# Window attention on one core: P times V with V stationary in four column groups, P streamed in fp32, and the products in another order

## The chip, the core and the metric

The kernel runs on one core of a Trainium2 chip. The core has a matrix engine (PE, or TensorE, whose weight loads the profile lists apart as PEld), a vector engine (DVE), an activation engine (ACT), a general engine (POOL, or GpSimd) and a queue for transfers (SP). They run independently, each through its own list of instructions in order, and wait for each other on semaphores. The metric is the device time of one execution in microseconds.

## The reference

```python
def _L0_conv_ref(x, qkv_w, qkv_b, proj_w, proj_b):      # WH, WW = 7, 11; 8 heads of 24 channels
...
    xw = xw.reshape(Bnw, N, C)                           # N = 77 tokens in a window
    qkv = xw @ qkv_w + qkv_b
    q, k, v = jnp.split(qkv, 3, axis=-1)
...
    attn = jnp.einsum('bhnd,bhmd->bhnm', q, k) / jnp.sqrt(jnp.float32(hd)).astype(q.dtype)
    attn = jax.nn.softmax(attn, axis=-1)
    out = jnp.einsum('bhnm,bhmd->bhnd', attn, v)
    out = out.transpose(0, 2, 1, 3).reshape(Bnw, N, C)
    out = out @ proj_w + proj_b
...
x = x + _L0_conv_ref(_gn(x), ...)                        # x: (8, 56, 88, 192) fp32; _gn: group norm, 32 groups
```

An image of 56x88 positions with 192 channels is cut into windows of 7x11 positions. There are 8 images and 512 windows. All values are fp32.

## The kernel before

The statistics of the group norm come first: the whole input is read once. Then the main part works on one pair of windows at a time. This is one slot; there are 256. 16 windows (8 pairs, two strips of 8 windows) make a block of 14 image rows, which is loaded and stored as one. A loop of 14 turns holds 16 slots each (two blocks); the first and the last 16 slots, and those that fill and drain the pipeline, are written out around it.

The order of the work is written by hand. Each engine has a function `slot(base, s)` that issues its share of slot s, with `reach(engine, semaphore, count)` ahead of each step; steps of other pairs stand in the same slot, shifted by constants (`AV_LAG` and so on). In slot s PE does, in this order: the scores q k of pair s with q_hi and k_hi alone (`ps_s`, for the row maximum), the k projection of pair s+1 for the first four heads (`qk_projection(ps_k, 1, 0, ...)`), P times V of pair s-2 for its first window (`attention_output`), six transposes of o of pair s-4, k of s+1 for the other four heads, P times V for the second window, four matmuls that add the negated row maxima as one more row to q (`ps_q<-ident_aug,neg_max`), the output projection of a tile or two (`ps_b<-wp`), the transposed scores in three products, q of s+1, V of s+1 (`ps_a<-wv`), and transposes of the normalised input x further ahead (`ps_b<-ident,x_split`).

A matmul in fp16 takes one pass, so fp32 precision is made from two halves: a value is rounded to fp16 (`_hi`) and the remainder kept as a second fp16 (`_lo`), and a product is the sum of three: hi hi, hi lo, lo hi. `products` issues such a group of matmuls, so nearly all matmuls have its line, L676. Making the halves is the work of the other engines: DVE makes q_hi, q_lo, k_lo, v_hi and v_lo, ACT makes k_hi and p_hi (p is the exponential of the scores), POOL makes p_lo, and both halves of o and of x are shared between ACT and POOL.

P times V has P stationary, 77 tokens by 128 columns, and moves the 25 columns of one head of V, the last of them ones, so that the row sum comes out beside the head; three matmuls for each of 16 (window, head), 48 in all. DVE then takes the reciprocal of 16 row sums for each token (L617, 77x16), multiplies (L619), ACT and POOL split o into halves, PE transposes it, ACT copies the transposed halves to `oT`, and the projection takes them as its stationary operand. POOL adds the projection's bias to y beforehand (L370), DVE adds the product to y (L627).

The result of P times V and V itself share the bank `ps_a`; x transposes, o transposes and the projection share `ps_b`.

Of the kernel before, what the change touches and what calls it, by code (L numbers as in the profile page):

```python
# [27 lines left out]
F16 = mybir.dt.float16  # L28
# [34 lines left out]
AV_LAG = 2  # L63
O_LAG = AV_LAG + 1
T_LAG = O_LAG + 1
P_LAG = PAIRS + O_LAG
Y_LAG = PAIRS - 1
V_BUFS = 4
FULL = 128
PAD = FULL - TOK  # L70
AUG_ONE = 32768.0
# [5 lines left out]
def window_attention(nc, x, qkv_w, qkv_b, proj_w, proj_b, out):  # L77
# [4 lines left out]
    with ExitStack() as ctx:  # L82
# [10 lines left out]
        ones = sb("ones", [128, PART])  # L93
        wA, wB = sb("wA", [CA, 3 * CH]), sb("wB", [128, 3 * CH])
        pA, pB = sb("pA", [CA, CH]), sb("pB", [128, CH])
# [3 lines left out]
        wp = {k: sb(f"wp_{k}", [128, CH], F16) for k in PARTS}  # L99
        b_qk, aug, zeros = sb("b_qk", [128, 4]), sb("aug", [128, 4]), sb("zeros", [128, 4])  # L100
        bvA, bvB, b_proj = sb("bvA", [CA, 1]), sb("bvB", [CB, 1]), sb("b_proj", [1, CH])
        bvA_rep, bvB_rep = sb("bvA_rep", [CA, PART]), sb("bvB_rep", [CB, PART])
        bias_out = sb("bias_out", [PART, CH])
# [19 lines left out]
        oT = [sb(f"oT{p}", [128, 3, TILES, PART], F16) for p in range(2)]  # L123
# [8 lines left out]
        v_hi = [sb(f"v_hi{p}", [TOK, 2 * HEADS, HD + 1], F16) for p in range(V_BUFS)]  # L132
        v_lo = [sb(f"v_lo{p}", [TOK, 2 * HEADS, HD + 1], F16) for p in range(V_BUFS)]
        neg_max = sb("neg_max", [TOK, 4, NG, ROW_G], F32R)
        probs = sb("probs", [TOK, NG * 4 * TOK])
        p_hi = [sb(f"p_hi{p}", [TOK, NG * 4 * TOK + PAD], F16) for p in range(2)]
        p_lo = [sb(f"p_lo{p}", [TOK, NG * 4 * TOK + PAD], F16) for p in range(2)]
        recip = sb("recip", [TOK, 2 * HEADS, 1])
        o_sb = [sb(f"o_sb{p}", [TOK, 2, CH]) for p in range(2)]
        o_split = sb("o_split", [TOK, 2, 2 * CH], F16)  # L140
# [6 lines left out]
        ps_b16 = ps_b[:, :].bitcast(F16)  # L147
# [4 lines left out]
        pe_av, pe_oT, pe_proj, pe_xT = sem("pe_av"), sem("pe_oT"), sem("pe_proj"), sem("pe_xT")  # L152
        act_k, act_exp, act_xT = sem("act_k"), sem("act_exp"), sem("act_xT")
        act_p, act_o, act_oT, act_x = sem("act_p"), sem("act_o"), sem("act_oT"), sem("act_x")
        dve_max, dve_q_hi, dve_q = sem("dve_max"), sem("dve_q_hi"), sem("dve_q")
        dve_k, dve_v_hi, dve_v = sem("dve_k"), sem("dve_v_hi"), sem("dve_v")
        dve_norm, dve_recip = sem("dve_norm"), sem("dve_recip")
        dve_out = sem("dve_out")
        pool_p, pool_o, pool_x, pool_y = sem("pool_p"), sem("pool_o"), sem("pool_x"), sem("pool_y")
# [4 lines left out]

        dma_w, dma_bqk, dma_stat = sem("dma_w"), sem("dma_bqk"), [sem("dma_stat0"), sem("dma_stat1")]
# [40 lines left out]
        def xT_psum(c):  # L206
            at = 3 * c * PART
            return ps_b16[:, at:at + 3 * PART].rearrange("p (k v r) -> p k v r", k=3, v=WINS)

        def oT_tokens(buf, chunk, pair):  # L210

            v = oT[buf][:, chunk, :, :].rearrange("p c (v r) -> p v c r", v=WINS)
            return v[:, 2 * pair:2 * pair + 2, :, :]

        def oT_psum(chunk):
            at = 2 * chunk * TOKE
            return ps_b16[:, at:at + 2 * TOKE].rearrange("p (w n) -> p w n", w=2)[:, :, 0:TOK]\
                .rearrange("p w (c r) -> p w c r", c=WIN_W)
# [13 lines left out]
        def _(sp):  # L232
# [3 lines left out]
            sp.dma_start(pA[:, :], proj_w[0:CA, :]).then_inc(dma_w, 16)  # L236
            sp.dma_start(pB[0:CB, :], proj_w[CA:CH, :]).then_inc(dma_w, 16)
            sp.dma_start(pB[CB:128, :], proj_w[CA:CH, :]).then_inc(dma_w, 16)
            v_bias = qkv_b[2 * CH:3 * CH].rearrange("(c a) -> c a", a=1)
            sp.dma_start(bvA[:, :], v_bias[0:CA, :]).then_inc(dma_w, 16)  # L240
            sp.dma_start(bvB[:, :], v_bias[CA:CH, :]).then_inc(dma_w, 16)
            sp.dma_start(b_proj[:, :], proj_b.rearrange("(a c) -> a c", a=1)).then_inc(dma_w, 16)

            sp.wait_ge(pool_const, 6)
            qk_bias = qkv_b[0:2 * CH].rearrange("(sj g d) -> g d sj", g=NG, d=HD)
            for g in range(NG):
                sp.dma_start(b_qk[ROW_G * g:ROW_G * g + HD, :], qk_bias[g, :, :],
                             allow_slow_non_contiguous=True).then_inc(dma_bqk, 16)
                sp.dma_start(aug[ROW_G * g:ROW_G * g + HD, 2:4], zeros[ROW_G * g:ROW_G * g + HD, 0:2])\
                    .then_inc(dma_bqk, 16)  # L250
# [8 lines left out]
            for h in range(2):  # L259
                load_half(0, h, 0)  # L260
            with sp.Fori(1, BATCH) as b:
# [48 lines left out]
        def _(pool):  # L310
# [7 lines left out]
            pool.wait_ge(pool_const, 6)  # L318
# [18 lines left out]
            def slot(base, s, image):  # L337
                i = base + s
                if exists(i - 1):

                    reach(pool, act_p, i)
                    reach(pool, pe_av, i - 2)
                    nc.gpsimd.tensor_tensor(p_lo[(s - 1) % 2][:, 0:16 * TOK], probs[:, :], p_hi[(s - 1) % 2][:, 0:16 * TOK],  # L343
                                            ALU.subtract).then_inc(pool_p, 1)
                if exists(i - O_LAG):

                    reach(pool, act_o, i - O_LAG + 1)
                    nc.gpsimd.tensor_tensor(o_split[:, :, CH:2 * CA], o_sb[(s - O_LAG) % 2][:, :, CA:CH], o_split[:, :, CA:CH],
                                            ALU.subtract)
                    nc.gpsimd.tensor_tensor(o_split[:, :, 2 * CA:3 * CA], o_sb[(s - O_LAG) % 2][:, :, 0:CA], o_split[:, :, 0:CA],  # L350
                                            ALU.subtract).then_inc(pool_o, 1)
# [8 lines left out]
                if exists(i + NORM_LEAD) and (s + NORM_LEAD) % PAIRS == 0:  # L360

                    reach(pool, dma_x[ahead % 2], base + 16 * (ahead // 2) + 16)
                if exists(i - Y_LAG):

                    r = s - Y_LAG
                    if r % PAIRS == 0:
                        reach(pool, dma_y[parity(r)], base + (r // SLOTS) * 16 + 16)
                    y = x_step(y_blk, r)
                    bias = bias_out[:, :].unsqueeze(1).broadcast_to([PART, STEP_TILES[r % PAIRS][1], CH])
                    nc.gpsimd.tensor_tensor(y, y, bias, ALU.add).then_inc(pool_y, 1)  # L370
# [21 lines left out]
        def _(act):  # L392
# [5 lines left out]
            def slot(base, s):  # L398
                i = base + s
                if exists(i - 1):  # L400

                    reach(act, act_exp, i)
                    reach(act, pe_av, i - 2)
                    nc.scalar.activation(p_hi[(s - 1) % 2][:, 0:16 * TOK], probs[:, :], ACT.Copy).then_inc(act_p, 1)  # L404
                if exists(i - T_LAG):

                    o = s - T_LAG
                    reach(act, pe_oT, i - T_LAG + 1)
                    for chunk in range(3):
                        last = nc.scalar.activation(oT_tokens(parity(o), chunk, o % PAIRS), oT_psum(chunk), ACT.Copy)  # L410
                    last.then_inc(act_oT, 1)
                if exists(i - O_LAG):

                    reach(act, dve_norm, i - O_LAG + 1)
                    nc.scalar.activation(o_split[:, :, 0:CH], o_sb[(s - O_LAG) % 2][:, :, :], ACT.Copy)\
# [435 lines left out]
```

## Time and profile before

| | us |
|---|---|
| median of 2 runs | 2115.62 (2107.02 to 2124.22) |
| the profiled execution | 2107.97 |
| its span | 2105.9 |
| mean granted clock of TensorE, 1 is 2.4 GHz | 0.937 |
| first exponential of the scores starts at | 213.0 |
| last one starts at | 2069.7 |

The profile is one execution. Its span is the time from the first to the last instruction; the execution is 2.1 us longer. Up to 160 us DVE reads the input for the statistics and PE has next to nothing to do; from 213 us on all engines repeat the slot.

### The profile page before, as it was taken

The page shows a single profiled execution, that of the slowest core. Times are in us where ns is not written, and L with a number is a line of the kernel's source. Part 1 is how long each engine was busy: PE and PEld are TensorE (multiplying, and loading weights), DVE is VectorE, ACT ScalarE, POOL GpSimd, SP SyncE. Part 2 cuts the span into 40 slices and gives each one's busy share as a digit, 9 for nine tenths or more (in the row PEclk, how much of TensorE's full clock was granted, in tenths as well). Part 3 has the DMA queues.
Part 4 walks back from the last instruction along what each step waited for, and adds up shares of the span by engine and source line. Part 5 has one row for each costly group of instructions (what it writes and reads, how often), then busy time and mean ns, then how long its engine had stood idle before and what let it go on. Part 6 is the DMA issues. An engine that isn't in the chain of part 4 may idle for free.

```text
span 2105.9 us, 97027 instructions
## 1 busy us (share of the span) xinstructions
PE 1691.6 (80%) x41742; PEld 1500.7 (71%) x41742; DVE 1515.2 (72%) x3672; ACT 1299.1 (62%) x2659; POOL 1608.9 (76%) x2060
## 2 busy tenths in 40 slices
PE   0003899988898888988898989988898889988886
PEld 0002788877787778877787878777787778887775
DVE  6772677777677776777777777777777777777783
ACT  0002667767676676766676766766676666767763
POOL 0004689888888898888888998988888888988864
PEclk9999899999999998999999998999999999999996
DMA  6881101111111111111111111111111111111110
GB/s 159 226 232 39 45 20 51 46 57 40 38 57 57 56 57 57 42 54 40 41 54 57 57 57 57 57 39 57 39 50 46 57 57 57 57 48 48 39 39 38
DMA packets 17134, 127.74 MB, mean 61 GB/s; under 512 B 1921, under 2 KB 2178, under 8 KB 2434
## 3 DMA queue, kind: packets, MB, share of 16 engines
q1 hardware_dynamic: 16770, 121.91, 17.1%
q8 instruction: 348, 5.70, 1.1%
q14 instruction: 16, 0.13, 0.0%
HBM read 91.62 MB, written 30.28 MB: 58 GB/s over the span
## 4 chain that ended last, share of the span: by engine, by line
PE 58%; DVE 26%; issue 10%; DMA 3%; ACT 1%; POOL 1%; DVEq 1%; SPq 0%; ACTq 0%; POOLq 0%
PE ps_a L676 25%; PE ps_q L676 8%; PE ps_q L775 6%; PE ps_k L676 6%; PE ps_s L715 6%; DVE v_lo L587 5%; DVE v_hi L641 5%; DVE q_lo L588 5%; DMA x_stat<-in_x 3%; PE ps_b L761 3%; DVE y_blk L627 2%; PE ps_b L676 2%; DVE q_hi L634 2%; DVE k_lo L588 2%; DVE stat L541 2%
## 5 line engine op out<-in xcount | busy, mean ns | idle before, releaser
L343 POOL TENSOR_TENSOR p_lo<-probs,p_hi 77x1232 f16<-77x1232 f32 x256 | 646.8, 2526 | 220.2 <-ACT p_hi L404 217.0
L434 ACT ACTIVATE probs<-ps_s,exp_shift,exp_scale 77x1232 f32<-77x1232 f32 x256 | 351.8, 1374 | 258.1 <-PE ps_s L715 246.1
L676 PE MATMUL ps_a<-v_hi,p_hi 77*128 77x25 f16 x4096 | 362.8, 174 | 84.6 <-DVE v_lo L587 81.9
L676 PEld LDWEIGHTS ps_a<-v_hi,p_hi 77*128 77x128 f16 x4096 | 330.1, 97 | 124.4 <-issue 122.0
L588 DVE SCALAR_TENSOR_TENSOR q_lo<-ps_q,b_qk,q_hi 128x154 f16<-128x154 f32 x512 | 170.4, 376 | 327.9 <-PE ps_q L775 327.9
L596 DVE TENSOR_REDUCE neg_max<-ps_s 77x16 fp32r<-77x1232 f32 x256 | 365.8, 1429 | 34.5 <-PE ps_s L730 34.5
L676 PE MATMUL ps_a<-v_hi,p_lo 77*128 77x25 f16 x4096 | 361.6, 174 | 0.0
L676 PE MATMUL ps_a<-v_lo,p_hi 77*128 77x25 f16 x4096 | 361.2, 174 | 0.0
L676 PEld LDWEIGHTS ps_a<-v_lo,p_hi 77*128 77x128 f16 x4096 | 323.3, 97 | 0.0
L676 PEld LDWEIGHTS ps_a<-v_hi,p_lo 77*128 77x128 f16 x4096 | 321.8, 97 | 0.0
L404 ACT ACTIVATE p_hi<-probs 77x1232 f16<-77x1232 f32 x256 | 310.0, 1211 | 0.3
L376 POOL TENSOR_TENSOR x_norm<-x_norm,mean_all 112x192 f32<-112x192 f32 (+1 forms) x256 | 165.9, 648 | 162.4 <-DVE rstd_all L581 162.4
L442 ACT ACTIVATE xT<-ps_b 128x336 f16<-128x336 f16 x352 | 171.5, 522 | 182.6 <-PE ps_b L829 182.6
L410 ACT ACTIVATE oT<-ps_b 128x154 f16<-128x154 f16 x768 | 181.5, 324 | 146.6 <-PE ps_b L761 144.8
L676 PE MATMUL ps_a<-wv_hiA,xT 128*128 128x192 f16 x1024 | 230.3, 263 | 0.0
L676 PE MATMUL ps_k<-xT,wqk_hiA 128*128 128x154 f16 x1024 | 198.7, 241 | 13.1 <-ACT xT L442 13.1
L378 POOL TENSOR_TENSOR x_norm<-x_norm,rstd_all 112x192 f32<-112x192 f32 (+1 forms) x256 | 166.0, 649 | 48.7 <-POOL x_norm L376 48.7
L634 DVE TENSOR_SCALAR q_hi<-ps_q,b_qk 128x154 f16<-128x154 f32 x512 | 167.8, 369 | 48.6 <-PE ps_q L676 48.4
L676 PE MATMUL ps_q<-xT,wqk_hiA 128*128 128x154 f16 x1024 | 200.5, 248 | 0.0
L715 PE MATMUL ps_s<-q_hi,k_hi 25*128 25x77 f16 x4096 | 145.9, 203 | 59.9 <-DVE q_lo L588 54.5
L370 POOL TENSOR_TENSOR y_blk<-y_blk,bias_out 112x192 f32<-112x192 f32 (+1 forms) x256 | 189.2, 740 | 0.0
L588 DVE SCALAR_TENSOR_TENSOR k_lo<-ps_k,b_qk,k_hi 128x154 f16<-128x154 f32 x512 | 168.0, 371 | 27.6 <-ACT k_hi L421 27.6
(147 smaller groups left out, 5693.5 us busy)
## 6 DMA issues: line engine op xcount, KB each, us to landing
x_stat<-in_x SPq DMA_DIRECT2D x16, 1848.0 KB, 9.9
x_norm<-in_x SPq DMA_DIRECT2D x32, 924.0 KB
y_blk<-in_x SPq DMA_DIRECT2D x32, 924.0 KB
out<-y_blk SPq DMA_DIRECT2D x32, 924.0 KB
wA<-in_qkv_w SPq DMA_DIRECT2D x1, 288.0 KB
wB<-in_qkv_w SPq DMA_DIRECT2D x2, 144.0 KB
pA<-in_proj_w SPq DMA_DIRECT2D x1, 96.0 KB
pB<-in_proj_w SPq DMA_DIRECT2D x2, 48.0 KB
```

What stands on the lines that cost most here:

```text
L343: nc.gpsimd.tensor_tensor(p_lo[(s - 1) % 2][:, 0:16 * TOK], probs[:, :], p_hi[(s - 1) % 2][:, 0:16 * TOK], ALU.subtract).then_inc(pool_p, 1)
L370: nc.gpsimd.tensor_tensor(y, y, bias, ALU.add).then_inc(pool_y, 1)
L378: nc.gpsimd.tensor_tensor(x4, x4, of_group(rstd_all, b, n), ALU.mult).then_inc(pool_norm, 1)
L404: nc.scalar.activation(p_hi[(s - 1) % 2][:, 0:16 * TOK], probs[:, :], ACT.Copy).then_inc(act_p, 1)
L410: last = nc.scalar.activation(oT_tokens(parity(o), chunk, o % PAIRS), oT_psum(chunk), ACT.Copy)
L434: nc.scalar.activation(probs[:, :].rearrange("p (g a n) -> p g a n", g=NG, a=4), scores(), ACT.Exp, bias=exp_shift[0:TOK, :], scale=exp_sc ...
L442: last = nc.scalar.activation(xT_tokens(parity(s + X_LEAD), t0 + c), xT_psum(c), ACT.Copy)
L588: return nc.vector.scalar_tensor_tensor(out=dst, in0=psum, scalar=bias, in1=hi, op0=ALU.add, op1=ALU.subtract)
L596: nc.vector.tensor_reduce(neg_max[:, :, :, HD:HD + 1].rearrange("p a g e -> p g (a e)"), scores(), AXIS.X, ALU.max, negate=True).then_inc( ...
L634: last = ts(by_window(q_hi, j), by_window(ps_q, j), b_qk[:, j:j + 1], None, ALU.add)
L676: last = mm(dst, lhsT, rhs, start=first and n == 0, stop=closes and n == len(pairs) - 1, skip_group_check=True)
L715: last = mm(ps_s[:, g, at:at + TOK], k[rows(g), a:a + FULL], q[rows(g), a:a + TOK], start=n == 0, stop=n == 2)
```

## The change

**P times V.** V is made in fp32 in one copy by ACT (`v_all`, 32 columns for each head: 24 of V, a one, seven zeros). It is now the stationary operand, 77x32, and P moves in fp32, 77 columns. The four heads g = 0 to 3 of a half go to the PSUM partitions 32g to 32g+31, each its own column group of the array. The result is o transposed, with channels on partitions, for both windows 308 columns. Since the row sum is needed on every partition, `denominators` multiplies a block of ones by P as well: eight matmuls that move 154 columns each, into `ps_b`.

**After it.** DVE takes the reciprocal of 128x308 sums and multiplies 128x308; ACT rounds the product into `oT_hi`, POOL makes `oT_lo`. There is no transpose of o any more, and P is no longer split. The projection takes three products for each half of the heads, six matmuls for a tile where there were five. Its bias comes in with the matmul: two spare rows of `wp_hi` hold it, against the ones and their remainder. POOL's addition of the bias is gone.

**The order.** P times V is one slot behind (`AV_LAG` 1, was 2), whole, after q of the next pair. Both halves of k stand behind the scores. V of pair s, not s+1, is made in slot s, ahead of the neg_max matmuls, and the projection stands ahead of V. The transposes of x go to k's bank. On DVE the reciprocal and the product stand first in the slot.

```diff
-AV_LAG = 2
+AV_LAG = 1
...
-                        last = products(ps_a[:, h * (HD + 1):(h + 1) * (HD + 1)], (
-                            (p_hi[p_now][:, at:at + FULL], v_hi[v_now][:, h, :]),
-                            (p_hi[p_now][:, at:at + FULL], v_lo[v_now][:, h, :]),
-                            (p_lo[p_now][:, at:at + FULL], v_hi[v_now][:, h, :])))
+                        at = (2 * w + j) * TOK
+                        o = ps_a[ROW_G * g:ROW_G * (g + 1), 2 * j * TOK:2 * (j + 1) * TOK]\
+                            .rearrange("p (c w r) -> p c w r", c=WIN_W, w=2)[:, :, w, :]
+                        last = mm(o, v_all[s % V_BUFS][:, HEADS * w + NG * j + g, :], probs[s % 2][:, g, at:at + TOK],
+                                  start=True, stop=True, skip_group_check=True)
+                return last
+
+            def denominators(s):
+
+                for w in range(2):
+                    for g in range(NG):
+                        d = ps_b[ROW_G * g:ROW_G * (g + 1), 0:NUM].rearrange("p (a w r) -> p a w r", w=2, r=WIN_H)
+                        last = mm(d[:, :, w, :], ones[0:TOK, 0:ROW_G], probs[s % 2][:, g, 2 * w * TOK:2 * (w + 1) * TOK],
+                                  start=True, stop=True, skip_group_check=True)
                 return last
```

On DVE, at the head of the slot, where the neg_max reduce stood first:

```diff
+                if exists(i - O_LAG):
+
+                    reach(dve, pe_av, i - O_LAG + 1)
+                    reach(dve, act_oT, i - O_LAG - 1)
+                    reach(dve, pool_oT, i - O_LAG - 1)
+                    nc.vector.reciprocal(den_inv[:, :], ps_b[:, 0:NUM]).then_inc(dve_recip, 1)
+                    reach(dve, dve_recip, i - O_LAG + 1)
+                    tt(o32[(s - O_LAG) % 2][:, :], ps_a[:, 0:NUM], den_inv[:, :], ALU.mult).then_inc(dve_norm, 1)
```

On PE, ahead of k, ahead of the projection, and around P times V:

```diff
+                    if exists(i - 1 + X_LEAD):
+
+                        reach(pe, act_xT, i + X_LEAD)
                     reach(pe, dve_k, i + 1)
                     qk_projection(ps_k, 1, 0, s + 1)
...
+                    if exists(i - O_LAG):
+                        reach(pe, dve_recip, i - O_LAG + 1)
...
+                    reach(pe, dve_norm, i - O_LAG + 1)
...
+                if exists(i - AV_LAG):
+
+                    reach(pe, act_exp, i - AV_LAG + 1)
+                    if exists(i):
+                        reach(pe, act_v, i + 1)
...
+                    attention_output(s - AV_LAG, 0)
+                    attention_output(s - AV_LAG, 1)
+                    if exists(i - P_LAG):
+                        reach(pe, dve_out, i - P_LAG + 1)
...
+                    denominators(s - AV_LAG).then_inc(pe_av, 1)
```

PE's list in one slot, from the end of P times V to the transposed scores (`ps_s<-q`; `ps_b<-wp` is the projection), before:

```order
L676 MATMUL ps_a<-v_lo,p_hi 128x25
L676 MATMUL ps_a<-v_hi,p_lo 128x25
L775 MATMUL ps_q<-ident_aug,neg_max 128x78 x4
L676 MATMUL ps_b<-wp_hiA,oT 112x192
...
L676 MATMUL ps_b<-wp_loB,oT 112x192
L715 MATMUL ps_s<-q_hi,k_hi 128x77 x4
```

and the same place after:

```order
L654 MATMUL ps_a<-wv_hiB,xT 128x192
L654 MATMUL ps_a<-wv_loB,xT 128x192
L766 MATMUL ps_q<-ident_aug,neg_max 128x78 x4
L701 MATMUL ps_s<-q_hi,k_hi 128x77 x4
```

Between neg_max and the transposed scores the projection stood, and now nothing does; V stands in front of neg_max. The end of the slot after, from q of the next pair over P times V (`ps_a<-probs`) and the row sums (`ps_b<-probs`) to k:

```order
L654 MATMUL ps_q<-xT,wqk_loB 128x2x77
L678 MATMUL ps_a<-probs,v_all 32x11x7 x16
L174 REGISTER_ALU
L687 MATMUL ps_b<-probs,ones 32x22x7 x8
L174 REGISTER_ALU x2
L808 MATMUL ps_k<-ident,x_split 128x112 x3
L716 MATMUL ps_s<-k_hi,q_hi 128x77 x16
L654 MATMUL ps_k<-xT,wqk_hiA 128x2x77
```

Before, V stood behind q and the two halves of P times V stood around the second half of k; now they are one piece of 24 matmuls in V's old place. DVE's list for one slot, before:

```order
L596 TENSOR_REDUCE neg_max<-ps_s 77x4x4
L588 SCALAR_TENSOR_TENSOR q_lo<-ps_q,b_qk,q_hi 128x2x77 x2
L588 SCALAR_TENSOR_TENSOR k_lo<-ps_k,b_qk,k_hi 128x2x77 x2
L617 RECIPROCAL recip<-ps_a 77x16
L619 TENSOR_TENSOR o_sb<-ps_a,recip 77x384
L627 SCALAR_TENSOR_TENSOR y_blk<-ps_b,out_scale,y_blk 112x384
L634 TENSOR_SCALAR q_hi<-ps_q,b_qk 128x2x77 x2
L641 CAST v_hi<-ps_a 77x16x24
L587 TENSOR_TENSOR v_lo<-ps_a,v_hi 77x16x24
```

and after:

```order
L585 RECIPROCAL den_inv<-ps_b 128x308
L587 TENSOR_TENSOR o_1<-ps_a,den_inv 128x308
L591 TENSOR_REDUCE neg_max<-ps_s 77x4x4
L600 SCALAR_TENSOR_TENSOR y_blk<-ps_b,out_scale,y_blk 112x192
L575 SCALAR_TENSOR_TENSOR q_lo<-ps_q,b_qk,q_hi 128x2x77 x2
L575 SCALAR_TENSOR_TENSOR k_lo<-ps_k,b_qk,k_hi 128x2x77 x2
L621 TENSOR_SCALAR q_hi<-ps_q,b_qk 128x2x77 x2
```

Reciprocal and product moved from behind k_lo to ahead of the neg_max reduce and have 308 columns; the two operations on V are gone.

## Rows read from the trace of the kernel before

**Rows 1.** The page: busy time by engine, and the clock in 40 slices.

```profile
PE 1691.6 (80%) x41742; PEld 1500.7 (71%) x41742; DVE 1515.2 (72%) x3672; ACT 1299.1 (62%) x2659; POOL 1608.9 (76%) x2060
...
PEclk9999899999999998999999998999999999999996
```

**Rows 2.** Chain of waits in order of time, one slot: start, us, what.

```profile
1206.77 0.48 PE ps_q L775 x4
...
1208.01 0.60 PE ps_s L715 x48
1208.61 0.79 PE ps_q L676 x10
1209.40 0.94 PE ps_a L676 x10
...
1210.36 0.57 DVE v_hi L641
...
1210.95 0.57 DVE v_lo L587
...
1211.65 0.76 PE ps_a L676 x24
1212.41 0.22 PE ps_b L761 x6
1212.63 0.34 PE ps_k L676 x5
1212.97 0.60 PE ps_a L676 x24
1213.57 0.48 PE ps_q L775 x4
```

**Rows 3.** The exponential's line: ns min/median/max, first and last start in us.

```profile
L434 ACT ACTIVATE probs<-ps_s,exp_shift,exp_scale x256: 1373/1374/1377, 213.0 to 2069.7; 77x1232 f32<-77x1232 f32 x128
```

**Rows 4.** Timeline of PE at a turn of the loop: start, us, what.

```profile
437.98 0.32 PE L730 MATMUL ps_s<-k_hi,q_hi 25*128 25x77 f16 x16 [3.33 <-issue]
```

**Rows 5.** Busy time by engine in three stretches; PEclk is the granted clock.

```profile
435.00:438.00 3.00, 0.03 (x4) 0.06 (x8) 0.53 (x1) 1.66 (x3) 2.82 (x4) 1.00 0.02 5
441.60:445.00 3.40, 3.40 (x66) 3.05 (x66) 2.27 (x7) 1.51 (x2) 3.15 (x6) 0.50 0.02 5
448.80:452.20 3.40, 3.07 (x95) 2.69 (x92) 2.25 (x8) 2.49 (x8) 3.40 (x4) 1.00 0.02 5
```

**Rows 6.** Groups by shape: busy us, mean ns of one | idle before.

```profile
L343 POOL TENSOR_TENSOR p_lo<-probs,p_hi 77x1232 f16<-77x1232 f32 x256 | 646.8, 2526 | 220.2 <-ACT p_hi L404 217.0
L596 DVE TENSOR_REDUCE neg_max<-ps_s 77x16 fp32r<-77x1232 f32 x256 | 365.8, 1429 | 34.5 <-PE ps_s L730 34.5
...
L442 ACT ACTIVATE xT<-ps_b 128x336 f16<-128x336 f16 x352 | 171.5, 522 | 182.6 <-PE ps_b L829 182.6
...
L619 DVE TENSOR_TENSOR o_sb<-ps_a,recip 77x384 f32<-77x384 f32 x256 | 141.7, 554 | 8.7
...
L617 DVE RECIPROCAL recip<-ps_a 77x16 f32<-77x16 f32 x256 | 62.5, 244 | 4.5 <-PE ps_a L676 4.5
...
L627 DVE SCALAR_TENSOR_TENSOR y_blk<-ps_b,out_scale,y_blk 112x384 f32<-112x384 f32 x96 | 58.0, 605 | 7.2 <-PE ps_b L676 7.2
...
L577 DVE RECIPROCAL rstd_all<-rstd_all 112x256 f32<-112x256 f32 x1 | 1.8, 1753 | 0.5 <-ACT rstd_all L395 0.5
```

**Rows 7.** Timeline of PE in the setup: start, us, what.

```profile
159.24 2.04 PE L663 MATMUL ps_q<-stat,ones 112*112 112x512 f32 x2 [138.45 <-DVE stat L541]
161.08 1.91 PE L663 MATMUL ps_k<-stat,ones 112*112 112x512 f32 x2
```

**Rows 8.** One line of the setup: ns min/median/max, first and last start.

```profile
L663 PE MATMUL ps_k<-stat,ones x2: 1053/1053/1053, 161.1 to 161.9; 112*112 112x512 f32 x2
```

**Rows 9.** Timeline within one slot.

```profile
1199.83 0.62 PE L775 MATMUL ps_q<-ident_aug,neg_max 77*128 77x78 f32 x4
...
1200.49 0.67 DVE L588 SCALAR_TENSOR_TENSOR q_lo<-ps_q,b_qk,q_hi 128x154 f16<-128x154 f32 x2 [1.23 <-PE ps_q L775]
```

More of the change, by code:

```diff
@@ L70 @@
 PAD = FULL - TOK
+NUM = 4 * TOK
+BIAS_ROOM = 1024.0
 AUG_ONE = 32768.0
@@ L122, in window_attention @@
         xT = [sb(f"xT{p}", [128, 3, COLS + PAD], F16) for p in range(2)]
-        oT = [sb(f"oT{p}", [128, 3, TILES, PART], F16) for p in range(2)]
+        oT_hi = [sb(f"oT_hi{p}", [128, NJ, TILES, PART], F16) for p in range(2)]
+        oT_lo = [sb(f"oT_lo{p}", [128, NJ, TILES, PART], F16) for p in range(2)]
         def sb_qk(name):
@@ L130, in window_attention @@
         k_lo = [sb_qk(f"k_lo{p}") for p in range(2)]
-        v_hi = [sb(f"v_hi{p}", [TOK, 2 * HEADS, HD + 1], F16) for p in range(V_BUFS)]
-        v_lo = [sb(f"v_lo{p}", [TOK, 2 * HEADS, HD + 1], F16) for p in range(V_BUFS)]
+        v_all = [sb(f"v_all{p}", [TOK, 2 * HEADS, ROW_G]) for p in range(V_BUFS)]
         neg_max = sb("neg_max", [TOK, 4, NG, ROW_G], F32R)
[L135 to L140, printed above, removed]
+        probs = [sb(f"probs{p}", [TOK, NG, 4 * TOK]) for p in range(2)]
+        den_inv = sb("den_inv", [128, NUM])
+        o32 = [sb(f"o32_{p}", [128, NUM]) for p in range(2)]
         ps_s = ctx.enter_context(nc.psum_tensor("ps_s", [128, NG, 512], F32))
@@ L338, in slot @@
                 i = base + s
[L339 to L344, printed above, removed]
-                if exists(i - O_LAG):
[L347 to L351, printed above, removed]
+                if exists(i - O_LAG):
+                    reach(pool, act_oT, i - O_LAG + 1)
+                    o = s - O_LAG
+                    nc.gpsimd.tensor_tensor(oT_tokens(oT_lo, o), by_column(o32[o % 2]), oT_tokens(oT_hi, o),
+                                            ALU.subtract).then_inc(pool_oT, 1)
                 if exists(i + SPLIT_LEAD):
@@ L360, in slot @@
                 if exists(i + NORM_LEAD) and (s + NORM_LEAD) % PAIRS == 0:
[L362 to L370, printed above, removed]
+                    passed(dma_x[ahead % 2], base + 16 * (ahead // 2) + 16)
                 if exists(i + NORM_LEAD):
@@ L464, in _ @@
             for p in range(V_BUFS):
-                nc.vector.memset(v_hi[p][:, :, HD:HD + 1], 1.0)
-                nc.vector.memset(v_lo[p][:, :, HD:HD + 1], 0.0)
+                nc.vector.memset(v_all[p][:, :, HD + 1:], 0.0)
+            for p in range(V_BUFS):
+                nc.vector.memset(v_all[p][:, :, HD:HD + 1], 1.0)
             for t in (q_hi, q_lo, *k_hi, *k_lo):
                 nc.vector.memset(t[:, :], 0.0)
-            for t in (*p_lo, *p_hi):
-                nc.vector.memset(t[:, NG * 4 * TOK:], 0.0)
             for p in range(2):
@@ L765, in slot @@
-                if exists(i + 1):
-                    qk_projection(ps_k, 1, 1, s + 1).then_inc(pe_k, 1)
-                if exists(i - AV_LAG):
-                    attention_output(s - AV_LAG, 1).then_inc(pe_av, 1)
+                    r = s - P_LAG
+                    if r % PAIRS == 0:
+                        reach(pe, pool_oT, i - P_LAG + PAIRS)
+                    t0, n = STEP_TILES[r % PAIRS]
+                    for c in range(n):
+                        hi, lo = oT_hi[parity(r)], oT_lo[parity(r)]
+                        passes = []
+                        for j in range(NJ):
+                            passes += [(hi[:, j, t0 + c, :], wp_hi[:, j, :]), (hi[:, j, t0 + c, :], wp_lo[:, j, :]),
+                                       (lo[:, j, t0 + c, :], wp_hi[:, j, :])]
+                        last = products(ps_b[0:PART, c * CH:(c + 1) * CH], passes)
@@ new lines, in slot @@
+                    last.then_inc(pe_proj, 1)
+                if exists(i):
+                    if s % PAIRS == 0:
+                        reach(pe, act_xT, i + PAIRS)
+                    reach(pe, dve_norm, i - O_LAG + 1)
+                    buf, pair = parity(s), s % PAIRS
+                    for w in range(2):
+                        at = (2 * pair + w) * TOK
+                        weights = {k: wv[k][:, :] for k in PARTS}
+                        last = products(ps_a[:, w * CH:(w + 1) * CH],
+                                        chunks(xT[buf][:, :, at:at + FULL], weights, True))
+                    last.then_inc(pe_v, 1)
```

243 lines of the change are left out of this document (99 added, 144 removed).

## The prediction

> **What bounds the kernel now.** I read the page first, then the chain of waits in order of time, then the groups by shape, and last the setup and one turn of the loop. On the page the reader is to see that no engine is full: PE 80%, POOL 76%, DVE 72% of the span [rows 1]. So the order of work within one pair of windows (one slot) matters, not a sum of busy time. The chain shows one slot in eleven pieces: from one neg_max matmul to the next there are 1213.57 - 1206.77 = 6.80 us [rows 2]. The reader is to see two kinds of time in it. PE works: transposed scores 0.60, q 0.79, V 0.94, the two halves of P times V 0.76 and 0.60, the six transposes of o 0.22, half of k 0.34, neg_max 0.48, 4.73 in all. The rest, 2.07, is DVE with PE's stream standing behind it: v_hi and v_lo, 0.57 each, 1.31 with their hand-overs (1210.34, where V ends, to 1211.65), and q_lo 0.76 (1207.25, where neg_max ends, to 1208.01). There are 256 slots. The first exponential starts at 213.0 and the last at 2069.7 [rows 3], so 255 periods take 1856.7 us. At 6.80 they would take 1734; 123 us are extra. They come mostly at the 15 passages from one group of 16 slots to the next (into, round and out of the loop; called turns here): PE stands still for 3.33 us with nothing to wait for but its own instructions [rows 4], and afterwards its granted clock is 0.50 (the 1.2 GHz level) where it was 1.00; in 3.40 us it then starts 66 matmuls against 95 in an equal stretch at 1.00 [rows 5].
>
> **What the change removes.** From PE per slot: 48 small matmuls (0.76 + 0.60) and six transposes (0.22), 1.58 us, all on the chain. From DVE: v_hi and v_lo, 1.31 us with their hand-overs, also on the chain, since V's product no longer has to be split before P times V can start. From POOL the subtraction p_lo at 2.53 us a slot [rows 6], from ACT p_hi and three oT copies, from POOL the bias; POOL and ACT are not on the chain, so this counts nothing. If that were all, the slot would be 6.80 - 2.89 = 3.91 us plus what comes in.
>
> **What it adds on PE.** Per slot 16 fp32 matmuls that move 77 columns and 8 that move 154. The nearest rows are the fp32 matmuls of the setup: each fp32 matmul shows as two matmul records. The second pair starts at 161.08, lasts 1.91, and each record takes 1.053 [rows 7, 8], so the records start 0.86 apart for 512 columns, 1.67 ns a column. PE had been idle for 138 us before, and rows at 0.50 follow an idle stretch [rows 5], so I take these as made at the 1.2 GHz level although the page has 9s there; at 2.4 GHz a record of 77 columns then takes 64 ns and one of 154 columns 128 ns. How far the four column groups stream beside each other no row shows. The ends: all four together, 4 rounds x 2 x 64 + 2 rounds x 2 x 128 = 1.03 us; nothing together, 16 x 128 + 8 x 256 = 4.1 us. Row groups do stream together: 48 score matmuls of 77 columns take 0.60 us, 12.5 ns each [rows 2]. But there the neighbours in the stream are always in different groups. Here the two records of one fp32 matmul stand next to each other in the same column group, so if matmuls start in order, the next group can start only with the second record: 64 ns for a matmul of 77 columns and 128 for one of 154, 16 x 64 + 8 x 128 = 2.05, with the hand-over 2.1 us. This is what I take; both ends stay in the range. A page of the Trainium skill bears on it: "TensorE: Matmul & The Clock Gate", Part 3 (packing small matmuls), says that column tiles run at the same time, three of them at 2.38 times the rate of one. By it alone the sum would be nearer the 1.03 end; no row here shows a column tile.
>
> **What it adds on DVE.** The normalisation now runs on the transposed output: a reciprocal of 128x308 in place of 77x16, then a product of 308 columns. Two reciprocals are in the trace: 16 columns take 244 ns and 256 columns 1753 ns [rows 6]. That is (1753 - 244) / 240 = 6.3 ns a column, against about 1.03 for other DVE work from PSUM (384 columns 554, 1232 columns 1429). So 308 columns take 244 + 292 x 6.3 = 2.08 us. The product takes about 554 - 76 x 1.03 = 0.48 us. The Trainium skill, "VectorE: DVE Perf Modes", says that the reciprocal is an iterated divide with a repeat count of 8, not an ordinary pass; the trace agrees in kind, with its 6.3 ns a column.
>
> **What it moves.** In DVE's stream reciprocal and product of the pair before last now stand ahead of the neg_max reduce of this pair, and they wait for the last matmul of PE's slot. Behind them on DVE are neg_max, y, q_lo; behind those on PE the neg_max matmul, the transposed scores, q, and P times V of this slot, whose last matmul releases the next reciprocal. That is a closed ring with nothing beside it:
> reciprocal 2.08, product 0.48, neg_max reduce 1.43 [rows 6], four neg_max matmuls 0.62, q_lo 0.67 [rows 9], transposed scores 0.60, q 0.79 [rows 2]: 6.67. Six hand-overs of about 0.05 (0.04 lies between the neg_max matmuls' end and q_lo's start in [rows 9]): 0.30. With P times V and the denominators at 2.1 the slot is 9.07 us.
> PE's other work lies beside DVE's 4.0 us: x transposes, scores, k, the output projection and V come to about 3 us. Scores must also wait for the exponential, which starts with q and takes 1.37 [rows 3], and is hidden by q and P times V. k now waits for the copy of xT by ACT (0.52 a tile [rows 6], one or two tiles), since x transposes now land in k's bank: some 0.4 to 0.8 us in which PE stands, but PE must wait for the reciprocal anyway before the projection (it overwrites the bank that the reciprocal reads), so it costs nothing as long as the reciprocal takes 2 us; without that cover it would be 0.4. The projection was behind neg_max and filled half of the q_lo wait; now nothing fills it, which is in the ring already. y stands on DVE between reduce and q_lo, 0.61 at most [rows 6], and PE's neg_max matmuls (0.62) hide it. k_hi and the copy of v on ACT, oT_lo on POOL are done beside the ring; both have more than 3 us of slack in 9. The setup gets a dozen small linked operations on DVE and the two row copies by DMA, 2 to 3 us; their DMAs stand on SP ahead of loads that wait for later work.
>
> **The sum,** against the profiled execution (2105.9 span and 2.1 around it): until the first exponential 213 + 3; 255 x 9.07 = 2313; the extra of turns and clock 125 as now; from the last exponential to the end 36 as now; 2 outside the span: 2692. The two times before have a median 0.4% above the profiled one, so 2700 us for the median. The turns might cost less (PE's 3.3 us now lie partly beside reciprocal and product, 15 x 1.9 = 28 less), and the clock might cost more; I leave the two against each other.
>
> **Rivals.**
> 1. All four column groups stream together, P times V is 1.03: the slot is 8.00, 255 x 1.07 = 273 less, 2430. For it: the score matmuls at 12.5 ns. Against: the pairs of records. Chance 0.22.
> 2. Nothing overlaps, 4.1: slot 11.07, 510 more, 3210. For it: fp32 rows here show no overlap at all. Chance 0.10.
> 3. The clock. PE now stands for some 2 us in every slot, and long stillness was followed by 0.50 [rows 4, 5]. At 1.2 GHz the pieces of the ring that PE streams could at most double, 0.62 + 0.60 + 0.79 + 2.1 = 4.1 more. A third of the slots so: 85 x 4.1 = 350 more, about 3000. Against: the gaps are under 1 us each, and at the turn it took 3.3. Chance 0.13.
> 4. The other side. The 6.3 ns come from a single SBUF row and a small one; if the long reciprocal from PSUM streamed at 1.03 ns a column it would take 0.5 and not 2.08, and with P times V under 1.03 too. Then PE's own work binds: with P times V at 1.03 about 7.0 us a slot (PE's 3 us of other work, 0.4 for xT, 0.62, 0.72, 1.39, 1.03, less what overlaps), 2170, 2.5% slower; with records at one column a clock, 0.5, about 6.5, 2040, faster by 3.6%. It decides from reciprocal and P times V together below 1.9 us (now 4.2). Against: both reciprocal rows lie on one line. Chance 0.05, of which 0.03 faster.
> That the change does not do what it says I give nothing: the order of the built program shows it.
>
> **How the numbers follow.** My forecast, 2600 to 2850, has 0.50. The range takes rivals 1 and 3 in and leaves 2 and 4 out: 2370 to 3010. Anything below 2% either way could not be told from no change here. Faster 0.03, same 0.03, slower 0.94.
>
> **What would show it.** Right: reciprocal rows of 2.1 us on DVE, a chain that runs reciprocal, product, neg_max, q_lo, scores, q, P times V, a slot near 9 us, P times V and denominators together 2.1 us at clock 1.00 with fp32 records some 64 and 128 ns apart, a POOL below 50%. Wrong: a reciprocal under 1 us, groups of four records within a few ns, a granted clock far below 0.9, or a chain in which ACT's copies of xT or v stand.

## The result, and the profile after

| | before | after |
|---|---|---|
| median of 2 runs, us | 2115.62 | 2487.79 (2479.41 to 2496.17) |
| the profiled execution | 2107.97 | 2479.41 |
| its span | 2105.9 | 2477.8 |
| mean granted clock | 0.937 | 0.921 |

The changed kernel takes 1.177 times as long, 95% interval 1.162 to 1.192. The page of after, busy time and clock, answers to [rows 1]:

```profile
PE 1750.1 (71%) x40558; PEld 1445.5 (58%) x40558; DVE 1730.2 (70%) x3161; ACT 990.7 (40%) x1891; POOL 717.7 (29%) x1294
...
PEclk9999699999899989999799989999899999998996
```

POOL's work fell from 1608.9 to 717.7 us, ACT's by 308, and no engine is near full: the kernel became longer because its engines wait for each other more. The chain of waits of after, in order of time (start, us, what), one slot, and the middle of a later one:

```profile
1000.77 2.09 DVE den_inv L585
...
1002.88 0.48 DVE o L587
1003.36 1.36 DVE neg_max L591
...
1004.76 0.65 PE ps_q L766 x4
...
1005.73 0.39 DVE q_lo L575
...
1006.16 0.60 PE ps_s L701 x48
1006.76 0.79 PE ps_q L654 x10
1007.55 0.68 PE ps_a L678 x32
1008.23 0.57 PE ps_b L687 x16
...
1008.83 2.10 DVE den_inv L585
...
1017.88 2.09 DVE den_inv L585
...
1020.01 1.20 PE ps_b L654 x12
1021.21 0.82 PE ps_a L654 x10
1022.04 0.49 PE ps_q L766 x4
```

From one reciprocal to the next there are 1008.83 - 1000.77 = 8.06 us, where [rows 2] had 6.80. (The slot behind it, up to 1017.88, is 9.05 long: in its projection PE stands for 0.91 us without a wait that the profile shows.) It is the ring that the prediction wrote down: reciprocal, product, neg_max reduce, neg_max matmuls, q_lo, transposed scores, q, P times V, sums. P times V takes 0.68 and the sums 0.57, 1.25 together. The last lines show a second way through the same slot: behind the reciprocal stands the projection, which overwrites its bank, then V, then the neg_max matmuls. From the reciprocal's start to that of the neg_max matmuls it takes 1022.04 - 1017.88 = 4.16, against 1004.76 - 1000.77 = 3.99 through DVE; the neg_max matmuls then take 0.49 instead of 0.65, so in a slot with two tiles to project both ways end together. The exponential's line, answering to [rows 3]:

```profile
L423 ACT ACTIVATE probs<-ps_s,exp_shift,exp_scale x256: 1373/1375/1379, 224.1 to 2440.9; 77x1232 f32<-77x1232 f32 x128
```

255 periods take 2216.8 us; at 8.06 they would take 2055, so 162 are extra, 123 before. The groups by shape, answering to [rows 6]:

```profile
L585 DVE RECIPROCAL den_inv<-ps_b 128x308 f32<-128x308 f32 x256 | 533.2, 2083 | 179.0 <-PE ps_b L687 179.0
...
L587 DVE TENSOR_TENSOR o<-ps_a,den_inv 128x308 f32<-128x308 f32 x256 | 122.5, 478 | 8.9
```

Where P times V begins, the timeline of PE, cut after 60 ns, has four matmul records beside each other:

```profile
1016.54 0.27 PE L678 MATMUL ps_a<-probs,v_all 77*32 77x77 f32 x4
```

The record starts in this slot are 1016.537, .544, .550 and .557, then four from 1016.628 on, four from .694, and so on: 32 records in eight rounds, the later rounds 66 to 71 ns apart. The sums follow in four rounds, 131 to 135 ns apart. One turn of the loop in the chain, answering to [rows 4]:

```profile
1050.43 2.80 issue
1053.23 0.41 PE ps_s L716 x13
1053.64 2.30 issue
...
1056.19 1.43 PE ps_k L654 x10
```

PE stands there for 2.80 and again for 2.30 us with nothing to wait for; in [rows 4] it was 3.33, once. Afterwards ten matmuls of k take 1.43 us, where 0.85 is usual: the 1.2 GHz level.

### The profile page after: what moved, and what is told of

It is laid out like the page before. It is cut to its first block, busy times and chain, and to the rows that moved or that the text cites. A ratio compares the mean times of both kernels' runs of the same rounds, so it can differ in the third digit from the quotient of the medians.

```text
span 2477.8 us, 91988 instructions
## 1 busy us (share of the span) xinstructions
PE 1750.1 (71%) x40558; PEld 1445.5 (58%) x40558; DVE 1730.2 (70%) x3161; ACT 990.7 (40%) x1891; POOL 717.7 (29%) x1294
## 4 chain that ended last, share of the span: by engine, by line
PE 51%; DVE 35%; issue 8%; DMA 3%; ACT 1%; POOL 1%; SPq 0%; DVEq 0%; POOLq 0%; ACTq 0%
DVE den_inv L585 19%; PE ps_q L654 8%; PE ps_a L678 8%; DVE neg_max L591 7%; PE ps_b L654 7%; PE ps_b L687 6%; PE ps_s L701 6%; PE ps_q L766 6%; PE ps_a L654 6%; DVE q_lo L575 5%; DMA x_stat<-in_x 3%; PE ps_k L654 2%; DVE o L587 2%; DVE stat L528 2%; PE ps_k L808 1%
## 5 line engine op out<-in xcount | busy, mean ns | idle before, releaser
L585 DVE RECIPROCAL den_inv<-ps_b 128x308 f32<-128x308 f32 x256 | 533.2, 2083 | 179.0 <-PE ps_b L687 179.0
L344 POOL TENSOR_TENSOR oT_lo<-o,oT_hi 128x308 f16<-128x308 f32 x256 | 193.0, 754 | 1487.8 <-ACT oT_hi L399 1487.8
L399 ACT ACTIVATE oT_hi<-o 128x308 f16<-128x308 f32 x256 | 119.8, 468 | 460.3 <-DVE o L587 406.8
L654 PE MATMUL ps_k<-xT,wqk_hiA 128*128 128x154 f16 x1024 | 201.7, 249 | 116.2 <-ACT xT L391 116.2
L701 PE MATMUL ps_s<-q_hi,k_hi 25*128 25x77 f16 x4096 | 139.3, 199 | 194.9 <-DVE q_lo L575 194.9
L391 ACT ACTIVATE xT<-ps_k 128x336 f16<-128x336 f16 x352 | 170.9, 521 | 264.5 <-PE ps_k L808 264.5
L654 PE MATMUL ps_b<-wp_hi,oT_hi 128*112 128x192 f16 x704 | 196.3, 279 | 84.8 <-DVE den_inv L585 78.4
L409 ACT ACTIVATE v_all<-ps_a 77x384 f32<-77x384 f32 x256 | 124.5, 486 | 254.2 <-PE ps_a L654 252.1
L678 PE MATMUL ps_a<-probs,v_all 77*32 77x77 f32 x8192 | 205.1, 243 | 0.0
L766 PE MATMUL ps_q<-ident_aug,neg_max 77*128 77x78 f32 x1024 | 171.1, 297 | 39.8 <-DVE neg_max L591 39.8
L687 PE MATMUL ps_b<-probs,ones 77*32 77x154 f32 x4096 | 198.4, 314 | 0.0
L654 PE MATMUL ps_b<-wp_lo,oT_hi 128*112 128x192 f16 x704 | 186.6, 265 | 3.1 <-issue 3.1
```

Source lines behind the costliest of these rows:

```text
L344: nc.gpsimd.tensor_tensor(oT_tokens(oT_lo, o), by_column(o32[o % 2]), oT_tokens(oT_hi, o), ALU.subtract).then_inc(pool_oT, 1)
L391: last = nc.scalar.activation(xT_tokens(parity(s - 1 + X_LEAD), t0 + c), xT_psum(c), ACT.Copy)
L585: nc.vector.reciprocal(den_inv[:, :], ps_b[:, 0:NUM]).then_inc(dve_recip, 1)
L654: last = mm(dst, lhsT, rhs, start=first and n == 0, stop=closes and n == len(pairs) - 1, skip_group_check=True)
L678: last = mm(o, v_all[s % V_BUFS][:, HEADS * w + NG * j + g, :], probs[s % 2][:, g, at:at + TOK], start=True, stop=True, skip_group_check=True)
L687: last = mm(d[:, :, w, :], ones[0:TOK, 0:ROW_G], probs[s % 2][:, g, 2 * w * TOK:2 * (w + 1) * TOK], start=True, stop=True, skip_group_chec ...
```

## The experiments

Each was run beside the kernel before, whose medians there were 2108.76, 2115.2 and 2118.36. Where no interval is given, the time is one execution. Slots are differences in the chain or the median period of the exponential. Lines with - are those of after unless another kernel is named.

**No reciprocal.** A pass of the same shape in its place; the kernel leaves out the division by the row sum.

```diff
-                    nc.vector.reciprocal(den_inv[:, :], ps_b[:, 0:NUM]).then_inc(dve_recip, 1)
+                    ts(den_inv[:, :], ps_b[:, 0:NUM], 0.0, 0.01, ALU.mult, ALU.add).then_inc(dve_recip, 1)
```

> The changed kernel with one pass of DVE over the same 128x308 sums (times 0, plus 0.01) in the place of the reciprocal. This leaves out the division by the row sums; all other instructions and waits stay. Theory (the ring of AV, reciprocal, product, neg_max, q_lo, scores, q sets the slot): 1.6 us go from the ring, the slot falls from 8.06 us to about 7.1, not to 6.5, because PE's own order (k waits for ACT's copy of xT, then projection, V, neg_max matmuls) then ends later than the ring; the time is near 2240 us. Rival (the slowdown is PE's: fp32 passes, the wait for xT, the gap at q_lo, and the reciprocal merely stands beside them): the slot stays above 7.8, over 2400 us.

Measured 2242.89 us, clock 0.934, median period 7.31. The pass takes 478 ns, so 1.61 us are gone from DVE, but only 0.75 from the slot. The chain says why:

```profile
1001.70 0.27 PE ps_k L808 x3
...
1001.99 0.53 ACT xT L391
...
1002.62 0.85 PE ps_k L654 x10
1003.46 0.49 PE ps_b L654 x6
1003.96 0.82 PE ps_a L654 x10
...
1008.98 0.91 ACT xT L391 x2
```

DVE's reciprocal and neg_max have left the chain, and PE's own list closes it, with a wait for ACT's copy of xT in the middle. So the ring set the slot of after, and the cover of the xT wait ends as the prediction said: "as long as the reciprocal takes 2 us". Without any reciprocal the kernel is still 6% slower than before (2242.89 against 2108.76), so the reciprocal alone does not make the loss: PE's own list in this order, with its wait for xT, needs 7.31 us, more than the 6.80 of before.

**Two neighbours in one column group.** The heads of a group behind each other, in P times V and in the sums.

```diff
-                for j in range(NJ):
-                    for g in range(NG):
+                for g in range(NG):
+                    for j in range(NJ):
```

> The changed kernel with the loops over heads and halves exchanged, in P times V and in the row sums: two matmuls that follow each other now go to the same column group, and the group changes after every second one. Same matmuls, same results. Theory (groups run side by side because neighbours in the list are in different groups): P times V with the row sums goes from 1.25 us to between 2.0 and 3.5, the slot from 8.06 to 9 to 10.3, the time to 2700 to 3050 us. Rival (PE takes matmuls of free groups ahead whatever their order): no change, 2480 us.

Measured 2486.28 us, slot 8.11. The chain of this kernel:

```profile
1005.84 0.71 PE ps_a L678 x32
1006.56 0.58 PE ps_b L687 x16
```

0.71 and 0.58 against 0.68 and 0.57: the theory was wrong, and the rival came. In strict order each group would stand for its own second matmul before the next one starts. It doesn't, so PE starts matmuls of free column groups ahead of one whose group is busy.

**Four neighbours in one column group.** How far does that reach? The sums go in twos, as in the kernel above.

```diff
-                for j in range(NJ):
-                    for g in range(NG):
+                for g in range(NG):
+                    for w, j in ((0, 0), (0, 1), (1, 0), (1, 1)):
```

> As the run with two neighbours in one group, now with all four matmuls of a column group behind each other in P times V. Same results. Theory (the order in the list does not matter, the four groups start within some ns whatever their order): within 0.1 us a slot of the changed kernel, 2480 to 2510 us. Rival (it reaches only a few matmuls ahead, so with four in a row the groups run one after another): P times V 1.5 to 2 us, 2700 us or more.

Measured 2762.12 us, clock 0.894, median period 8.91. The chain of this kernel:

```profile
1001.36 1.35 PE ps_a L678 x29
1002.71 0.07 PE ps_b L687
1002.78 0.07 PE ps_a L678
1002.85 0.59 PE ps_b L687 x11
```

P times V doubles to 1.35: the rival came, not the theory. In the records of this slot the first four start alone, at 1001.288, .379, .446 and .516. From the fifth on, at 1001.583, they come two at a time, the first two 6 ns apart, instead of four. So the reach is limited to some matmuls; where exactly it ends no run here shows. Three records of the sums start at 1002.489, .502 and .515, before the last three of P times V that the trace has, at 1002.551, .618 and .687, which stand ahead of them in the list. From 1001.36 to 1003.44 P times V and the sums take 2.08 where after has 1.25, which is the 0.85 that the slot is longer. The Trainium skill, "TensorE: Matmul & The Clock Gate", Part 3, says that matmuls keep program order in start and end; this trace disagrees for column groups, at least in the starts.

**All in one column group.** P times V into partitions 0 to 31; the output of the other heads is left out, and the sums stay as they are. One matmul ahead of the loop, not shown, fills the rest of the bank.

```diff
-                        o = ps_a[ROW_G * g:ROW_G * (g + 1), 2 * j * TOK:2 * (j + 1) * TOK]\
+                        o = ps_a[0:ROW_G, 2 * j * TOK:2 * (j + 1) * TOK]\
```

> The changed kernel with the 16 matmuls of P times V all written to the column group of partitions 0 to 31 (the attention output of the other heads is left out, its sums stay in four groups). This measures what the column groups bring. Theory (four groups stream together, each fp32 matmul of 77 columns takes 2 x 64 ns in its group): P times V goes from 0.68 to 2.05 us, the slot from 8.06 to 9.4, the time to about 2830 us. Rival (the groups bring little, the spacing comes from issue): under 1 us, below 2550 us.

Measured 2878.4 us, clock 0.938, slot 9.65. The chain of this kernel:

```profile
1000.78 2.19 PE ps_a L679 x31
1002.97 0.66 PE ps_b L688 x13
```

As expected. 32 records at 68 ns are 2.19 us: with one group nothing overlaps, and the whole difference lands in the slot (2.19 - 0.68 = 1.51, and 9.65 - 8.06 = 1.59). The four groups are worth a factor of 2.19 / 0.68 = 3.2. The same page of the Trainium skill, Part 3, has 2.38 for three column tiles; the trace agrees in kind.

**The reciprocal on ACT.** 1/x as exp(-ln x), two passes ahead of the copy of xT; DVE's product waits for them.

```diff
+            nc.scalar.preload_act_table_set("natural_log_exp_and_others")
...
+                    nc.scalar.activation(den_log[:, :], ps_b[:, 0:NUM], ACT.Ln).then_inc(act_log, 1)
+                    reach(act, act_log, i - O_LAG + 1)
+                    nc.scalar.activation(den_inv[:, :], den_log[:, :], ACT.Exp, scale=-1.0).then_inc(act_inv, 1)
...
-                    nc.vector.reciprocal(den_inv[:, :], ps_b[:, 0:NUM]).then_inc(dve_recip, 1)
-                    reach(dve, dve_recip, i - O_LAG + 1)
+                    reach(dve, act_inv, i - O_LAG + 1)
```

> The changed kernel with 1/sum as exp(-ln(sum)) on ACT, at the head of ACT's slot, nothing reordered. Theory (two bounds lie close together: the ring, and PE's own list with its wait for xT): the ring falls by 1.1 us to about 7.0, but ln and exp now stand ahead of the copy of xT that k waits for, so PE's list ends later: 7.6 us in slots with one tile, 8.4 with two, 2420 us. Rival (the ring alone decides): 7.0 us and about 2210 us.

Measured 2389.2 us, clock 0.935, median period 7.88. The chain of this kernel:

```profile
1001.02 0.44 ACT den_log L391
...
1001.48 0.46 ACT den_inv L393
1001.94 0.42 ACT xT L399
...
1002.45 0.85 PE ps_k L661 x10
```

The 2.08 us are down to 0.92, and DVE is off the chain; but the two passes now stand in front of the copy that PE's k waits for. 4% faster than after, still 13% slower than before.

**ln and exp, and another order.** On PE the neg_max matmuls ahead of V; on DVE the reduce first, the product behind it, y further back; on ACT the copy of xT ahead of ln, and k_hi ahead of the copy of v.

```diff
 # DVE: the reduce ahead of the product
+                if exists(i):
+
+                    reach(dve, pe_scores, i + 1)
+                    nc.vector.tensor_reduce(neg_max[:, :, :, HD:HD + 1].rearrange("p a g e -> p g (a e)"),
...
 # PE: ahead of V
+                if exists(i):
+
+                    reach(pe, dve_max, i + 1)
+                    for w in range(2):
```

> A version meant to beat both: 1/sum is made on ACT as exp(-ln(sum)) with one table set for both functions; DVE takes neg_max first, then the product, q_lo, k_lo, y, q_hi; PE does the neg_max matmuls ahead of V, so that V fills the wait for q_lo; ACT makes k_hi ahead of the copy of v. Theory (the ring through a 2.08 us reciprocal is what made it slow): slot 6.3 to 6.6 us, time near 2050 us, 3% faster than before the change. Rival (fp32 passes and lower clock cost more than the removed fp16 passes): slot above 7, 2200 us or more.

Measured 2002.69 us, median of 4 (1992.99 to 2021.14), ratio to before 0.948, 0.943 to 0.954; slot 6.49. PE's list of waits has one large entry left in the slots, 117.9 us for the copy of xT, in 233 places.

**The same order, the reciprocal back on DVE.** Reciprocal and product at the head of DVE's slot, no ln and exp; otherwise the kernel above.

```diff
-                    nc.scalar.activation(den_log[:, :], ps_b[:, 0:NUM], ACT.Ln).then_inc(act_log, 1)
...
-                    nc.scalar.activation(den_inv[:, :], den_log[:, :], ACT.Exp, scale=-1.0).then_inc(act_inv, 1)
...
+                    nc.vector.reciprocal(den_inv[:, :], ps_b[:, 0:NUM]).then_inc(act_log, 1)
```

> The order of the run before (neg_max matmuls ahead of V, y behind k_lo, k_hi ahead of v's copy), but with the reciprocal on DVE, at the head of the slot as in the changed kernel. Theory (the ring sets the slot, and PE's order stands beside it): the same 8.06 us a slot and about 2480 us, although V now fills the wait for q_lo. Rival (the empty wait for q_lo is what costs): the slot falls by up to 0.7 us, to 2300 us.

Measured 2596.79 us, slot 8.07 where nothing disturbs it, median period 8.75, clock 0.865. The slot was expected, the time was not. The ring is the same length as in after: V moved from ahead of neg_max to behind it, reciprocal, product and reduce still stand in line. The rest goes with the clock. A line of PE's waits in this kernel (us in total, times, longest):

```profile
PE ps_q L754 <- DVE neg_max L591: 215.4, 223, 2.3
```

In after that wait had 39.8 us in 123 places. PE's three large waits in these slots add up to 413 us (215.4, 116.1 and 81.1), its four in after to 429 (194.9, 116.2, 78.4 and 39.8). About the same idle time, in other places of the slot, goes with 703 us at 0.50 in place of 392. That the places are the cause is not shown, and two kernels from above speak against a simple rule. The kernel with ln and exp in the old order has its idle time in two places, 194.8 us at q_lo and this line:

```profile
PE ps_k L661 <- ACT xT L399: 240.5, 236, 2.4
```

It is at 0.50 for only 314 us. The kernel with four neighbours has the waits of after (194.9, 114.0, 37.4, and this line) and is at 0.50 for 587:

```profile
PE ps_b L654 <- DVE den_inv L585: 72.1, 142, 2.2
```

**The reduce ahead of the reciprocal.** After with DVE's first steps exchanged.

```diff
+                if exists(i):
+
+                    reach(dve, pe_scores, i + 1)
+                    nc.vector.tensor_reduce(neg_max[:, :, :, HD:HD + 1].rearrange("p a g e -> p g (a e)"),
...
                     nc.vector.reciprocal(den_inv[:, :], ps_b[:, 0:NUM]).then_inc(dve_recip, 1)
```

> The changed kernel with the neg_max reduce ahead of reciprocal and product on DVE, nothing else moved. Theory (the ring is closed by PE's list too: the projection waits for the reciprocal and V for the product, and both stand ahead of the neg_max matmuls): from the end of the row sums scores 0.6, reduce 1.43, reciprocal 2.08, product 0.48, V 0.99, then the neg_max matmuls: 5.6 where it was 4.2, so the slot goes from 8.06 to 9.4 and the time to about 2840 us. Rival (with the reduce out of the way early, DVE's 2 us stand beside PE's work and the slot gets shorter): under 8 us, below 2450 us.

Measured 3594.42 us, clock 0.613, median period 13.23, the shortest 9.8 once the pipeline is full. The sign was expected, the size was not: at 9.8 the 255 periods would take 2504 us, near the theory, and they take 3332. The chain, and a line of PE's waits:

```profile
999.92 2.08 DVE den_inv L590
...
1002.04 2.17 PE ps_b L654 x12
...
1005.81 0.77 PE ps_q L766 x4
...
1009.71 1.19 PE ps_a L678 x32
1010.90 1.03 PE ps_b L687 x16
```
```profile
PE ps_b L654 <- DVE den_inv L590: 473.6, 247, 3.5
```

The pieces that PE streams take 1.6 to 1.95 times what they take in after (2.17 against 1.20, 1.19 against 0.68), and the reciprocal takes what it always takes. The stretch of 14.2 us from 999.9 has a granted clock of 0.54, and 2781 of the 3593 us are at the 1.2 GHz level. What holds the clock down is not settled; what is shown is that this kernel's PE stands in one piece of 1.9 us on average in 247 slots (473.6 / 247), and that after, with 78.4 us in 148 places for the same wait, is at 0.50 for 392 us.

**The transposes of x ahead of P times V.** In the kernel with ln and exp and the new order, so that ACT's copy runs beside P times V.

```diff
+                if exists(i + X_LEAD):
...
                 if exists(i - AV_LAG):
...
                     denominators(s - AV_LAG).then_inc(pe_av, 1)
-                if exists(i + X_LEAD):
```

> The faster order of before with the transposes of x ahead of P times V instead of behind it, so that ACT copies xT while PE does P times V, and k need not wait. Theory (in that version PE waits for xT in every slot and x transposes stand in front of the scores on the ring): 0.25 us less in slots with one tile, 0.5 in those with two; slots of 5.8 and 6.0 us, near 1920 us, 9% faster than before the change. Rival (the neg_max reduce and its hand-overs bound the front of the slot anyway, the wait only moves): under 0.1 us gained, 2000 us.

Measured 1921.1 us, median of 4 (1915.31 to 1927.73), ratio to before 0.909, 0.902 to 0.915; clock 0.954. The chain of this kernel:

```profile
1005.62 1.45 DVE neg_max L591
...
1007.12 0.64 PE ps_q L761 x4
1007.76 0.84 PE ps_a L661 x10
...
1009.92 0.30 PE ps_k L799 x6
1010.22 0.68 PE ps_a L685 x32
1010.90 0.53 PE ps_b L694 x16
...
1011.73 1.45 DVE neg_max L591
```

6.11 us from one reduce to the next; of DVE only the reduce is left in the chain, and the wait for xT is gone. This is the fastest of all kernels here: the arithmetic of the change with another place for the reciprocal and another order is 9% faster than before.

## Why the prediction was right, and where it was off

The range, 2370 to 3010, holds the measured 2487.79. Its likeliest part, 2600 to 2850, with a chance of 0.50, does not: what came is rival 1, put at 2430 with 0.22. One of the prediction's own signs of being wrong, groups of four records within a few ns, is in the trace.

**The ring: right.** It was to run reciprocal, product, reduce, neg_max matmuls, q_lo, scores, q, P times V, and it does. Without P times V and the sums it was put at 6.97 and measures 8.06 - 1.25 = 6.81. Taking the reciprocal out shows that the ring, not PE's list, sets the slot of after, and that PE's list lies only 0.75 behind.

**The reciprocal: right.** 2.08 from two distant rows, 2083 ns measured; the product 0.48, measured 478 ns.

**P times V: the size was off.** The likeliest case had 2.1 us, rival 1 had 1.03, and 1.25 came. The step that failed is "the two records of one fp32 matmul stand next to each other in the same column group, so if matmuls start in order, the next group can start only with the second record". The records' length was right (64 and 128 ns, against rounds of 66 to 71 and 131 to 135), though by an assumption: the prediction halved rows of the setup as made at the 1.2 GHz level, and the trace has no record of the clock before 209.8 us. The order was not right: four first records start within 20 ns, and then the four second ones. With two neighbours in one group it is still 0.71, with four 1.35, with all sixteen 2.19. So rival 1 is what happened, with some 0.2 us on top of its 1.03.

**The sum.** Against 2692 for the profiled execution: P times V 255 x 0.85 = 217 less; the rest of the ring 255 x 0.16 = 41 less; until the first exponential 224.1 for 216, 8 more; the extra of turns and clock 162 for 125, 37 more; the end 1 more. 2692 - 217 - 41 + 8 + 37 + 1 = 2480, measured 2479.41.

**The turns and the clock: left against each other, and they did not cancel.** A turn in after has a period of 13.9 to 16.4 us, 6 to 8 over the slot, for 10.0 to 11.4 before, some 4.2 over. There are 13 such turns, not 15: the periods at the first and the last passage are 6.8 and 6.8 before, 8.2 and 8.1 after. Added up, the 13 turns are 55 us over the slot before and 89 after. That is 34 of the 39 us by which the extra grew. Of the 123 us before, "mostly at the 15 passages" covers 55 in the turns themselves; 64 lie in slots at a lower clock, some behind a turn and some far from one. The discount of 1.9 a turn was wrong in sign: PE stands 5.1 us there, not 3.3. The cause of the second piece was not tried. The clock was rival 3, a third of the slots at 0.50, 350 us more. After is at 0.50 for 392 us, before for 267, but outside the turns the slots with a mean granted clock below 0.95 are together 67 us over the usual length in after, 64 before. So the clock cost next to nothing more. The kernels at 0.894, 0.865 and 0.613 show that it can cost much in this design; what decides it stays open. (By the prediction's own numbers rival 3 comes to 3050, not 3000.)

**"So it costs nothing as long as the reciprocal takes 2 us": right.** Without the cover the copies stand in the chain with 0.53 for one tile and 0.91 for two, more than the 0.4 that the prediction named for that case.

**PE's other work "lies beside DVE's 4.0 us": true, but with nothing to spare.** The projection and V behind the reciprocal take 4.16 in a slot with two tiles. This is why shortening DVE alone gave 0.75 us of 1.61.

**Setup: 11 us more, for 2 to 3.** DVE's last step of the statistics ends at 180.4, 1.9 later than before. The rest is POOL, the timeline of after:

```profile
188.18 0.85 POOL L362 TENSOR_TENSOR x_norm<-x_norm,mean_all 112x384 f32<-112x384 f32 x1 [171.61 <-issue]
```

It starts 7.8 us later than DVE ends, and before 0.1 us later; the page names no wait. The trace has an instruction there that the views leave out, MODIFY_POOL_CONFIG. Before, it ran at 16.2 us, while POOL still had to wait for the statistics; in after it runs at 180.64 and 180.67, behind that wait, 7.5 us before the subtraction starts. In the nine other kernels it runs at 177.8 to 180.5, also behind the wait, and the subtraction starts 6.8 to 7.5 us later. So some 7 of the 11 us go with the place of this instruction; no run moves it back.

## What to carry to other kernels

Write down the closed ring of hand-overs first, and price in it every operation by its shape: here 2.9 us left the chain, and 4.0 us on DVE came in, over half of them a reciprocal that moved from 16 columns to 308. But one experiment is not the cause whole: without the reciprocal the kernel was still 6% slower than before, bound by the order of PE's list. When a cheaper place is found for such an operation, look at once at what else stands in line behind and ahead of it; here the place alone gave 4%, and the order around it another 20% (2389.2 to 1921.1). Look at the granted clock of each variant before comparing their times: two kernels with the same matmuls and the same ring had 0.921 and 0.865. Which placing of PE's idle time keeps it up these runs do not settle.

## What the runs showed of the hardware

- DVE's reciprocal takes 2083 ns for 308 columns, 1753 for 256, 244 for 16: 6.3 ns a column, whatever it reads from. Another pass of 308 columns takes 478.
- ACT does the same in two passes, ln 427 ns and exp 460 ns in the fastest kernel, with 8.2 us of idle time ahead of all 256 exps together. The Trainium skill, "ScalarE: Activation LUTs", What it computes, sends a reciprocal to VectorE, for accuracy; on time the runs here speak for ACT.
- fp32 matmuls in four column groups run beside each other, four records in 20 ns, and PE draws matmuls of free groups forward over a limited distance: sixteen take 0.68 us alternating, 0.71 in twos, 1.35 in fours, 2.19 in one group.
- The granted clock of a whole kernel was 0.613 where PE stood about 2 us in one piece in nearly every slot. It also was 0.894 with the same waits of PE as in a kernel at 0.921, so idle time alone does not tell it.
- POOL started its first subtraction 6.8 to 7.5 us after MODIFY_POOL_CONFIG in all ten kernels in which that instruction ran behind the wait for the statistics.
